# Window attention and routed experts on one core: score products in 32-row by 64-column tiles, gates spread over partitions by DMA, and a new stage order

## What is computed

```
xn  = ln_c(x)                              # layer norm over the 64 channels
q, k, v = windows of 8x8 tokens of xn @ w_qkv.T, 4 heads of 16 channels
attn = softmax(q @ k.T * 0.25 + bias)      # 64x64 per window and head
x = x + (attn @ v) @ w_proj.T + b_proj
t = ln(x); p = softmax(t @ router_w + router_b)          # 8 experts
top_p, top_i = top_k(p, 2);  top_p = top_p / sum(top_p)
x = x + sum over the 2 of top_p * (t @ expert_w[i] + expert_b[i])
```

## Time and profile before

| | |
|---|---|
| time of three runs (median; lowest to highest) | 1442.63 us; 1441.42 to 1443.07 |
| span of the profiled execution, first to last instruction | 1442.2 us |
| PE, busy | 1343.6 us, 93% |
| PE weight loads, busy (they overlap the products) | 749.6 us, 52% |
| DVE, busy | 1161.9 us, 81% |
| ACT, busy | 862.6 us, 60% |
| POOL, busy | 356.8 us, 25% |
| DMA, mean share of its engines; moved | 17.6% on the kernel's queue; 72.89 MB |
| granted PE clock, mean | 0.976 |

### The profile page before, as it was taken

One profiled execution on the slowest core, in us unless ns is written; L12 is line 12 of the kernel. 1 busy time (PEld: TensorE's weight loads), 2 busy tenths in 40 slices (PEclk: granted clock), 3 DMA queues, 4 the chain that ended last, 5 costly groups with the idle time before them and its releaser, 6 DMA issues.

```text
span 1442.2 us, 32800 instructions
## 1 busy us (share of the span) xinstructions
PE 1343.6 (93%) x11179; PEld 749.6 (52%) x11332; DVE 1161.9 (81%) x2398; ACT 862.6 (60%) x1729; POOL 356.8 (25%) x488
## 2 busy tenths in 40 slices
PE   5779999999998999989999999989999899999987
PEld 3555555555554555555555555545555555555531
DVE  4468888888887888878888788878888788888774
ACT  2576666566665666656666566656666566666530
POOL 2013222331232232122233132222123223213221
PEclk6899999999999999999999999999999999999998
DMA  4011211212221211221121222121222121221110
GB/s 156 1 45 30 60 40 50 60 31 60 60 60 32 60 45 45 60 61 45 45 60 31 60 60 59 35 57 30 60 60 60 31 60 40 51 60 45 45 44 30
DMA packets 20931, 72.89 MB, mean 51 GB/s; under 512 B 3600, under 2 KB 3856, under 8 KB 20624
## 3 DMA queue, kind: packets, MB, share of 16 engines
q1 hardware_dynamic: 20752, 70.60, 17.6%
HBM read 20.25 MB, written 16.78 MB: 26 GB/s over the span
## 4 chain that ended last, share of the span: by engine, by line
PE 69%; ACT 10%; DVE 10%; issue 9%; POOL 1%; DMA 1%; DVEq 0%; ACTq 0%; SPq 0%; POOLq 0%
PE bank L378 14%; PE bank L514 12%; PE bank L388 7%; PE bank L462 6%; PE bank L502 5%; ACT vbd L680 5%; PE bank L417 4%; PE bank L374 4%; PE bank L404 4%; DVE z L899 3%; PE bank L410 2%; PE bank L491 2%; PE bank L484 2%; PE bank L436 2%; DVE mx L879 2%
## 5 line engine op out<-in xcount | busy, mean ns | idle before, releaser
L899 DVE TENSOR_TENSOR z<-bank,xd 128x512 f32<-128x512 f32 x512 | 329.2, 683 | 15.4 <-PE bank L502 9.3
L514 PE MATMUL bank<-z,wcen 128*64 128x512 f32 x1024 | 284.7, 621 | 4.6 <-issue 0.3
L587 ACT ACTIVATE probs<-shifted 128x512 f32<-128x512 f32 x256 | 161.5, 631 | 208.0 <-DVE shifted L882 205.7
L378 PE MATMUL bank<-kex,qbd 128*128 128x256 f32 x1024 | 269.2, 386 | 0.0
L879 DVE TENSOR_REDUCE mx<-bank 128x8 f32<-128x512 f32 x256 | 176.1, 688 | 108.9 <-PE bank L378 107.4
L378 PEld LDWEIGHTS bank<-kex,qbd 128*128 128x128 f32 x1024 | 198.8, 194 | 25.6
L767 POOL TENSOR_TENSOR tt<-prj,xs 128x512 f32<-128x512 f32 x64 | 81.2, 1268 | 457.6 <-DVE z L899 287.9
L882 DVE TENSOR_TENSOR shifted<-bank,mx 128x512 f32<-128x512 f32 x256 | 177.1, 692 | 9.8
L388 PE MATMUL bank<-cst,probs 128*128 128x128 f32 x1024 | 157.7, 277 | 24.9 <-issue 16.8
L595 ACT ACTIVATE pt<-bank 128x512 f32<-128x512 f32 x256 | 150.7, 589 | 46.0 <-PE bank L388 43.0
L388 PEld LDWEIGHTS bank<-cst,probs 128*128 128x128 f32 x1024 | 124.5, 142 | 77.2 <-issue 38.9
(11 more groups left out here) (116 smaller groups left out, 1998.2 us busy)
## 6 DMA issues: line engine op xcount, KB each, us to landing
xd<-tt SPq DMA_DIRECT2D x128, 256.0 KB, 4.0
xs<-in_x SPq DMA_DIRECT2D x32, 512.0 KB, 4.8
out<-ob SPq DMA_DIRECT2D x32, 512.0 KB, 3.1
kex<-in_rel SPq DMA_DIRECT2D x1, 2048.0 KB, 9.4
tt<-in_select SPq DMA_DIRECT2D x1, 512.0 KB, 8.9
cst<-in_consts SPq DMA_DIRECT2D x1, 359.0 KB, 2.8
tt<-in_weights SPq DMA_DIRECT2D x1, 336.0 KB, 3.1
wproj<-in_proj SPq DMA_DIRECT2D x1, 64.0 KB, 8.2
```

Source lines behind the costliest of these rows:

```text
L378: last = mm(b[:, 256 * j:256 * j + 256], qbd[s.buf(2)][:, w, :, :].rearrange("p a q -> p (a q)"), kex[s.buf(2)][:, w, :, :].rearrange("p h ...
L514: mm(bank[64 * a:64 * a + 64, Y_BANK, :], wcen[:, WE + C * j:WE + C * j + C], z[n % 4][:, :], start=False, stop=(j == 3), skip_group_check ...
L587: af(probs[u % 2][:, :, :].rearrange("p w k -> p (w k)"), shifted[u % 2][:, :, :].rearrange("p g k -> p (g k)"), ACT.Exp).then_inc(exp_don ...
L899: tt_(z[n % 4][:, :], bank[:, G_BANK[n % 2], :], xd[s.buf(2)][:, a, c * CH:(c + 1) * CH], op=ALU.mult).then_inc(z_ready, 1)
```

## The change

The score products take each head by itself. A head pair lies in 32 partitions, so `scores(h)` now makes half a strip in one burst: four bias products into four banks, then for each of 8 windows four products with 32 contraction rows, 64 weight columns and 128 moving columns, one in each 32-row part of the array, each row part writing to its own bank. `softmax_shift`, `exps` and the probabilities work by group (1024 columns) and no longer by unit (512), and the subtraction writes into `probs`, where `exps` works in place. `kex` and `kr` go: `move_k` on ACT writes the keys twice with a mask (`km`). `qs`, `km` and `vbd` have one buffer each.

`gates_wide` goes. The gates are written to a DRAM scratch by SP, come back as 48 rows for the bias of the experts (`grow`, one fp32r product for half a strip), and come back again as 16 DMAs a strip, each of which spreads one row of gates over 64 partitions in `gz`. `gated` multiplies `gz` by `xd` in place, both images in one instruction, 8 times a strip. The experts' products stay as they are. A fifth strip (`fin`, strip c-3) takes part in each step with the last three items, and there is one step more, to c = 34. The slots are laid out anew on all engines.

```diff
-            def scores(st, u):
...
-                wait(pe, shift_done, s.count(UNITS, u - 1))
-                mm(b, tile_id[:, :], dup(bias_hl[:, :, :].rearrange("p h k -> p (h k)")), start=True, stop=False,
-                   skip_group_check=True)
-                for j in range(2):
-                    w = 2 * u + j
-                    last = mm(b[:, 256 * j:256 * j + 256], qbd[s.buf(2)][:, w, :, :].rearrange("p a q -> p (a q)"),
-                              kex[s.buf(2)][:, w, :, :].rearrange("p h k -> p (h k)"), start=False, stop=(j == 1),
-                              skip_group_check=True)
+            def scores(s, h):
+                pe.wait_ge(q_ready, s.count(2, h + 1))
+                pe.wait_ge(k_ready, s.count(4, 2 * h + 2))
+                wait(pe, shift_done, s.count(GROUPS, 2 * h))
+                for r in range(4):
+                    mm(bank[:, r, :], tile_id[:, :],
+                       bias_hl[:, 2 * (r % 2):2 * (r % 2) + 2, :].rearrange("p h k -> p (h k)").unsqueeze(1).broadcast_to(
+                           [P, 4, 2 * N]), start=True, stop=False, skip_group_check=True)
+                for i in range(4):
+                    for j in range(2):
+                        w = 8 * h + 2 * i + j
+                        for r in range(4):
+                            last = mm(bank[N * j:N * j + N, r, 2 * N * i:2 * N * i + 2 * N], qs[32 * r:32 * r + 32, w, :],
+                                      km[32 * r:32 * r + 32, w, :, :].rearrange("p m k -> p (m k)"),
+                                      start=False, stop=(i == 3), skip_group_check=True)
                 last.then_inc(s_full, 1)
...
+            def spread_gates(s, n):
+                c, j = n // 4, n % 4
+                wait(sp, e_done, s.count(ITEMS, n + 1, lag=1))
+                by_expert = gates_dram[s.buf(2), 0].rearrange("(a e) t -> e a t", a=2)
+                for e2 in range(2):
+                    sp.dma_start(gz[64 * e2:64 * e2 + 64, n, :, :],
+                                 by_expert[2 * j + e2, :, c * CH:(c + 1) * CH].partition_broadcast(64)
+                                 ).then_inc(gz_loaded[n], 16)
...
-                tt_(z[n % 4][:, :], bank[:, G_BANK[n % 2], :], xd[s.buf(2)][:, a, c * CH:(c + 1) * CH],
+                tt_(gz[:, n, :, :], gz[:, n, :, :], xd[s.buf(2)][:, :, c * CH:(c + 1) * CH],
                     op=ALU.mult).then_inc(z_ready, 1)
...
+                    if k in (0, 3, 8, 11) and att.on:
+                        softmax_shift(att, (0, 3, 8, 11).index(k))
+                    if k in (0, 2) and fin.on:
+                        gated(fin, 6 + k // 2)
                     if k == 1 and pre.on:
                         variance(pre)
-                    if k == 2 and old.on:
-                        normalise(old, 3)
                     if k == 2 and pre.on:
                         low_part(pre)
+                    if k == 4 and old.on:
+                        normalise(old, 3)
```

543 lines of the change are left out of this document (248 added, 295 removed).

## The result

The changed kernel takes 2040.84 us (median of four runs, 2037.4 to 2048.59) against 1442.85 us of the kernel before on the same chip: ratio 1.414, 95% interval 1.410 to 1.417. It is slower by 598 us, inside the predicted range, and 132 us above the predicted 1909.

The account below looks back on a forecast made before the run. In-order waits that PE's work no longer covers bound the new kernel: 28 steps of 57 us (1596), loop turns 20, up to step 3 190, last steps 103, together 1909 us; range 1,650 to 2,080.

Parts of the forecast that it names:

- Rival 1: The walked order's waits hold, with 53 to 62 us a step: 1,780 to 2,060 us; chance 0.70.
- The walk: One full step followed, each engine strictly in order: 55 us, with PE idle for 21.6.
- the five loop turns: Turns of the loop within steps 3 to 30: 4 us each for idle time and a slow restart, 20 together.
- the clock: PE at half clock behind its long waits: 2 us added to the walked 55, so 57 a step, ends 55 and 60.
- 33.5 us of work: PE's busy time in a step of the new order, summed from prices of its parts.
- The burst: Half a strip's score products on PE: four bias products 1.0 us and 32 tile products 2.2, so 3.2.
- DMA at nothing: A strip's 16 gate spreads, 4 MB: priced at nothing, hidden under the walk's own waits.
- The meeting: DVE's gated and POOL both reading SBUF: priced at 0.1 to 0.5 us; by the skill's rule possibly over 1.
- Rival 2: Part of the waits isn't real: 43 to 52 us a step, 1,470 to 1,760 us; chance 0.13.
- 4: Row tiles run one after another on PE: 7.9 us a burst, 66 us a step, about 2,170 us; chance 0.07.
- 5: Spreads don't share the DMA queue: 64 us a step one by one, about 68 with the chain, some 2,230; chance 0.05.
- Rival 3: Faster: waits hide under PE's 33.5 us, 34.5 a step, 1,255 us, given normalise(old, 3) early enough; chance 0.04.

Follow-up runs that it names:

- e1: Changed kernel with the strip's last normalise moved earlier on DVE, its inverse sums and the first transposed copy earlier on ACT; 1913.75 us, ratio 1.324.
- e5: Kernel before with one line moved: normalise(old, 3) later on DVE, behind the key masks of slot 3; 1529.85 us, ratio 1.061.
- e12: Last of several rounds of reordering the changed kernel, against the round of 1481.52 us: second score burst ahead of the projection, other moves; 1395.46 us, ratio 0.966.
- e4: Changed kernel with useless zero-weight products on PE (20, 11, 8 and 6) ahead of four long waits of a step; 1932.86 us, ratio 1.339.
- e2: Changed kernel without the 16 spreading DMAs a strip, gates left out of the result; 2023.58 us, ratio 1.401.
- e10: Reordered version of 1568.36 us with its eleven places of PE waits treated by further moves on PE, DVE and ACT; 1508.81 us, ratio 1.046.
- e7: e1 with four more moves on DVE, ACT and PE, no useless work; 1706.5 us, ratio 1.183.
- e8: e7 with useless products as well (8, 11, 8, 6 in slots 6 to 12); 1740.73 us, ratio 1.208.

## Why the prediction was right, and where it was off

**The mechanism.** Rival 1 came true, step by step. The walk let PE start the first values 15.95 us into the step, behind 5.2 us of idle time; the trace has them at 822.60, 15.79 us after slot 0 at 806.81, behind 5.88. The order of causes was the one walked: `high_std`, `low_part`, the softmax group, `normalise`. The agreement to 0.2 us is partly luck: DVE began the first softmax group 3.75 us into the step where the walk had 4.75, and the stages behind it took 0.8 us longer than walked. e1 and e5 show that this place is worth 127 us here and 86 us there.

**The sum.** 190 us up to step 3 were 194.6. The 28 steps with the loop's turns were put at 1596 + 20 = 1616 and took 1726.9 [the third row of the stretches above]. The last steps were put at 103 and took 114.1. Of the 127 us that the span lies above the sum, 111 are in the steps. Two errors stand against each other there. A step took 61.4 us for 57, above the 60 that I gave as its upper end; over 28 steps that is 125 us, and two steps were 3.5 us longer still (in the one from 440.27 PE was busy for 44.08 us, at a clock of 0.79). But the five loop turns, put at 20 us, cost nothing that shows: the step from 566.52 to 628.01, with a turn in it, took 61.5. The time lies in the range because rival 1 allowed steps up to 62 us.

**The term that was too small is the clock.** The walk without it gave 55 us, and 2 were added for it. PE's products of a step take 33.63 us at a granted clock of 1.00 (e12) and took 41.94 at 0.83, so the clock cost 8.3 us; the waits were 19.6 us where the walk had 21.6. With 33.5 us of work that makes 61.4. (The 33.5 was right by errors against each other: the pieces that I listed leave 32.5, and two bursts were 1.9 us too dear, so the rest was too cheap.) Single legs show it as well: slots 4 to 8 were walked in 13.9 us (15.95 to 29.85) and took 17.60, whose waits (1.24, 0.87, 1.47 and 3.00 us) are no longer than the walk's by more than 0.1:

```profile
822.60:840.20 17.60, 11.02 (x70) 4.90 (x71) 4.67 (x6) 6.36 (x13) 4.64 (x3) 0.79 1.06 248
```

From the values of slot 12 to the next step the walk has 9.3 us (45.8 to 55.1) and the trace 11.4 (857.03 to 868.43). I had let half clock follow only the wait of 5.2 us and a part follow that of 3.2. In the trace the clock is at 0.50 behind five places of a step: behind the waits of 5.88 and 3.00 us, behind single ones of 1.81 (849.62) and 1.45 us (857.03), and behind the chain of 1.24, 0.87 and 1.47 us, at whose start it had been 1.00 again (1.00 from 827 to 832, 0.50 from 834 to 835). The sums at 833.13, behind that chain, took 0.98 us where 0.61 is their time at full clock. e4 puts a price on it without any change of order, 3.4 us a step, and it had more to give. By the Trainium skill (TensorE: Matmul & The Clock Gate, Part 1: The HAM clock gate) the clock has two states, and the lower one is that of an idle engine; the traces agree, with granted clocks of 0.50 and 1.00.

**The burst was too dear.** I took 3.2 us; it took 2.27, and its 32 tile products 1.14 instead of 2.2. The bound from below, 1.6, was too high as well. The nearest row, four column tiles side by side, was not near: there 8 records of 0.38 us took 0.55, here 64 records of 0.27 us took 1.14, so nearly three times as many overlap. By the Trainium skill (TensorEngine Tiling, Key Properties and Theoretical Speedup), eight tiles at a time gave an estimate of 0.9 for the products and 1.9 for the burst; the trace lies between that and my value, nearer to the rule, and no drain of the size of a microsecond shows at the two changes of mode. In time it mattered little: e3 removes the products and wins 26 us.

**DMA at nothing** was right for the steps of this kernel (e2: 17 us over all). It was right for its reason, slack, and the slack can be used up: in e10, whose readers come earlier, DVE waited 76.5 us for the spreads.

**POOL and DVE.** The meeting was priced at 0.1 to 0.5 us. On DVE a product of gates, and on POOL `xr_low` with and without it beside:

```profile
832.25 1.22 DVE L887 TENSOR_TENSOR gz<-gz,xd 128x1024 f32<-128x1024 f32 x1
```

```profile
832.47 2.12 POOL L772 TENSOR_TENSOR xr_low<-xr,xr_high 128x512 fp32r<-128x512 f32 x1 [0.66 <-ACT xr_high L635]
838.95 1.26 POOL L772 TENSOR_TENSOR xr_low<-xr,xr_high 128x512 fp32r<-128x512 f32 x1 [4.35 <-ACT xr_high L635]
```

POOL came 0.22 us after DVE and was held for 0.86 us; DVE was not. In e7 POOL came first, and it was DVE's turn:

```profile
797.24 1.27 POOL L778 TENSOR_TENSOR xr_low<-xr,xr_high 128x512 fp32r<-128x512 f32 x1 [1.46 <-ACT xr_high L638]
```

```profile
797.39 2.20 DVE L893 TENSOR_TENSOR gz<-gz,xd 128x1024 f32<-128x1024 f32 x1
```

```profile
799.64 1.97 PE L521 MATMUL bank<-gz,wcen 128*64 128x512 f32 x4 [1.52 <-DVE gz L893]
```

So the one that comes second waits for nearly all that is left of the first; by the Trainium skill (SBUF — State Buffer, Who interferes with whom) that is the lock of the shared ports, and the traces agree. A meeting costs 0.9 to 1.0 us, above my upper value, but in this kernel it fell on POOL, about once a step, and no engine waited for `xr_low`. In e7 it fell on DVE, and PE's experts waited for that product: 1.0 of their 1.52 us are the meeting's.

**Rivals.** Rival 2 had its condition in part, a shorter burst and 2 us less of waits, but the clock took more than that back. 4 and 5 are refuted by the burst of 2.27 us and by e2. Rival 3, a faster kernel, is wrong for this order and right for its condition: it asked that `normalise(old, 3)` come early enough and that 13.5 of the 21.6 us of waits go, and e12 does both (5.3 us of waits are left in the step shown). It needed more than the rival said, though: not one early instruction, but nearly every meeting of a step; and its 1,255 us were not reached, as the mean step is 40.7 us and not 34.5.

## What to carry to other kernels

When a change takes work from the engine that ends last, ask first what that work was covering. Walk one step of the new order by hand, engine by engine: here it gave the place and size of the largest wait within 0.7 us. Then add for every wait the slow clock behind it, for waits of 1 to 2 us too: here that was 8 us of a step of 61.5. When the new parts are innocent (leave each out once), the cure is the order: put work whose inputs are ready ahead of each product that waits, let its producer go ahead of wide instructions nobody is waiting for, and look at the trace again after each round, since the next wait stands beside the one filled, and a transfer that was hidden may come out. Judge a round by the mean of all steps: in e12 single steps vary by 4 us.

## What the runs showed unexpectedly of the hardware

- 64 records of tile products (32 rows by 64 columns, 128 fp32 columns) take 1.14 us from the first start to the next product, 18 ns a record, though each record lasts 268.
- More work can take less time: 45 useless products a step made the kernel 108 us faster, at a clock of 0.926 for 0.835. Less work can take nearly as long: without the tile products the clock fell to 0.802. Where few waits are left, 33 useless products a step cost 34 us (e8).
- The stretch behind the long wait, 822.60 to 840.20, moved 248 GB/s at a DMA share of 1.06, and a spread of 256 KB took 7.7 us in the median to land, where `xd` of the same size took 4.0 before and 6.6 now; no engine waited for a spread in that stretch.
